# Graph aggregation with the weighting matrix as the stationary operand: node sums on the lanes, copied by ScalarE and transposed back, in groups of 896 edges with matrices of 128 columns

## The reference, cut to what matters

```python
def _gcn_layer(x, W, b, edge_weight, edge_src, edge_dst):
    support = x @ W
    msgs = support[edge_src] * edge_weight[:, None]
    agg = jax.ops.segment_sum(msgs, edge_dst, num_segments=N_NODES)
    return agg + b
h = jax.nn.elu(_gcn_layer(x, W1, b1, edge_weight, edge_src, edge_dst))
h = jax.nn.elu(_gcn_layer(h, W2, b2, edge_weight, edge_src, edge_dst))

...
x = x + _L0_gnn_ref(_layernorm(x, axis=-1), L0_gnn_W1, L0_gnn_b1, L0_gnn_W2, L0_gnn_b2, edge_weight, src, dst)
x = x + _L0_ffn_ref(_layernorm(x, axis=-1)[None], L0_ffn_W1, L0_ffn_b1, L0_ffn_Wg, L0_ffn_bg, L0_ffn_Wd, L0_ffn_bd)[0]
```

## Time and profile before

| | us |
|---|---|
| median of 3 runs | 4540.26 (4538.99 to 4540.56) |
| profiled execution, first to last instruction (span) | 5639.2 |
| profiled execution, anything around the span | not given |
| PE busy, share of the span | 3611.2, 64% |
| POOL busy, share of the span | 3287.1, 58% |
| DVE busy, share of the span | 2125.6, 38% |
| ACT busy, share of the span | 1218.9, 22% |

### The profile page before, as it was taken

The page is one execution under the profiler, slowest core; times in us unless marked ns, Lnnn a source line. Parts: engine busy times, 40 slices in busy tenths (PEclk is TensorE's granted clock), DMA queues, the critical chain, the costliest instruction groups (busy, mean ns, idle before and its releaser), DMA issues.

```text
span 5639.2 us, 84567 instructions
## 1 busy us (share of the span) xinstructions
PE 3611.2 (64%) x21407; PEld 3303.4 (59%) x21408; DVE 2125.6 (38%) x7215; ACT 1218.9 (22%) x2041; POOL 3287.1 (58%) x3464
## 2 busy tenths in 40 slices
PE   4555445555555545557667676666776776678998
PEld 3554444555544545456666666666666666667777
DVE  6663233223232322224334443333443433354332
ACT  4551110000000000013223232232232322232111
POOL 5666556666666666655565655555555555524555
PEclk6666666666666666668777777778777777789999
DMA  4543323333333333323333333333333333344444
GB/s 149 166 154 92 90 86 91 95 96 93 96 95 96 94 96 93 94 77 103 104 115 113 114 114 114 106 108 111 113 112 110 111 111 104 107 130 142 156 156 138
DMA packets 248031, 626.81 MB, mean 111 GB/s; under 512 B 66279, under 2 KB 113014, under 8 KB 247358
## 3 DMA queue, kind: packets, MB, share of 16 engines
q0 software_dynamic: 173664, 491.88, 30.3%
q1 hardware_dynamic: 69646, 103.75, 5.1%
q10 hardware_dynamic: 4176, 26.61, 1.3%
HBM read 519.22 MB, written 103.73 MB: 110 GB/s over the span
## 4 chain that ended last, share of the span: by engine, by line
PE 40%; issue 24%; another core or an unknown queue 4%; DVEq 4%; DVE 3%; DMA 2%; ACT 1%; POOL 0%; POOLq 0%; ACTq 0%; SPq 0%
PE pA L1381 18%; PE pB L1422 13%; PE pZ L1391 3%; PE pC L1404 3%; DMA aggT<-pay_scratch,ids 2%; PE pA L1536 1%; DVE S L927 1%; DVEq L927 1%; PE pZ L1415 1%; DVEq L953 1%; PE pT L1410 0%; DVE aggT L978 0%; PE pC L1526 0%; DVEq L978 0%
## 5 line engine op out<-in xcount | busy, mean ns | idle before, releaser
L1381 PE MATMUL pA<-S,rows 128*128 128x96 f32 x12544 | 1857.1, 312 | 961.7 <-issue 639.8
L1381 PEld LDWEIGHTS pA<-S,rows 128*128 128x128 f32 x12544 | 1797.0, 228 | 1039.1 <-issue 1033.8
L549 POOL DMA_INDIRECT rows<-h_scratch,idx x1564 | 1491.4, 954 | 1107.8 <-issue 424.2
L549 POOL DMA_INDIRECT rows<-xn_scratch,idx x1296 | 1227.9, 947 | 742.7 <-issue 366.2
L1422 PE MATMUL pB<-work,w 128*128 128x128 f32 x3232 | 776.5, 380 | 707.3 <-issue 702.3
L1422 PEld LDWEIGHTS pB<-work,w 128*128 128x128 f32 x3232 | 656.0, 279 | 818.9 <-issue 818.2
L927 DVE TENSOR_SCALAR S<-iota_p,tdst,twgt 128x96 f32<-128x96 f32 x3168 | 852.8, 351 | 288.2 <-issue 280.7
L978 DVE TENSOR_TENSOR aggT<-aggT,pA 128x192 f32 x784 | 278.0, 355 | 1340.3 <-remote 851.1
L1030 DVE TENSOR_TENSOR zb<-pZ,brow 128x256 f32<-128x256 f32 x198 | 84.0, 424 | 1150.0 <-issue 692.8
L1391 PE MATMUL pZ<-wg,stage 128*128 128x256 f32 x784 | 276.0, 485 | 213.0 <-ACT stage L642 126.2
L1536 PE MATMUL pA<-aggT,work 128*128 x1680 | 387.5, 384 | 10.8 <-DVE work L1311 10.1
(11 more groups left out here) (200 smaller groups left out, 2613.9 us busy)
## 6 DMA issues: line engine op xcount, KB each, us to landing
pay_scratch<-work SPq DMA_DIRECT2D x98, 512.0 KB
rows<-h_scratch,idx POOLq DMA_INDIRECT x1564
rows<-xn_scratch,idx POOLq DMA_INDIRECT x1296
work<-in_x_dram ACTq DMA_DIRECT2D x15, 896.0 KB
xn_scratch<-work ACTq DMA_DIRECT2D x14, 896.0 KB
h_scratch<-work SPq DMA_DIRECT2D x98, 128.0 KB
pay_scratch<-work SPq DMA_DIRECT2D x98, 128.0 KB
work<-in_x_dram SPq DMA_DIRECT2D x97, 128.0 KB
```

The costliest lines, as they stand in the source:

```text
L549: pool.indirect_dma_start(rows[:, s, t, :], None, source, bass.IndirectOffsetOnAxis(at, 0))\
L1381: last = mm(to[:, k * W:(k + 1) * W], rows[:, slot, t, k * P:(k + 1) * P], Sx[:, t, :], start=(t == 0), stop=(t == T - 1))
```

## The change

- Groups have 7 tiles (896 edges), 224 per layer; a half is 2 groups, 112 halves per layer; 4 slots for gathered rows instead of 8. The matrices have 128 columns.
- In the product `S` is the stationary operand and the gathered rows stream past, 256 columns, so the sums have nodes on the lanes (`group_products`). Both groups of a half share a bank of `pA`.
- ACT copies the sums of a half from PSUM to `gsum`, 512 columns (`copy_sums`), before its ticks; in the raw stage behind the normalising of the next half's rows. PE turns them with four transposes into the other bank of `pA` (`transpose_sums`), behind the half's ticks. DVE adds them to `aggT`, one instruction of 256 columns per group (`add_groups`).
- DVE builds the matrices of the next half ahead of its ticks, from a small copy of the table's columns (`tnext`), made two halves ahead, without register offsets.
- In the raw stage statistics, root, scales and normalising go by half (14 tiles) instead of by pair (8 tiles).
- At most `0.875 h + 3` blocks are due by half h (`PACE`).
- Tables of the start have rows of 896 edges, in two chunks of up to 128 groups instead of four.

The diff, cut to its core. The sizes, and ACT's part (the raw stage, the copy, the order behind the raw stage):

```diff
-    T = 4
+    T = 7
     GE = T * P
-    W = 96
-    SLOTS = 8
+    W = P
+    SLOTS = 4
+    PACE = 0.875
...
             def raw_half(i, half, with_chunk):
...
-                row_root(2 * h + 2, ahead)
-                row_normalise(2 * h + 2, ahead)
+                row_root(h + 1, ahead)
+                row_normalise(h + 1, ahead)
+                copy_sums(0, h)
                 if with_chunk:
                     chunk_normalise(h, half)
                     chunk_store(h, half)
                     chunk_root(h + 1)
-                row_root(2 * h + 3, ahead + 2)
-                row_normalise(2 * h + 3, ahead + 2)
...
+            def copy_sums(layer, h):
+                act.wait_ge(s_mm[layer], HALF * h + HALF + SLOTS)
+                act.activation(gsum[:, :], pG2, ACT.Copy).then_inc(s_gc[layer], 1)
...
                     for half in range(2):
                         h = 2 * i + half
+                        copy_sums(layer, h)
                         _, start, end = half_flags(act, layer, h)
                         ticks(act, start, end, lambda j: (tick1, tick2)[layer](j, h))
```

DVE's part (matrices, adds, the order in the raw stage and behind it):

```diff
+            def build_S(layer, h, buf):
+                dve.wait_ge(s_tab[layer], h + 1)
+                for u in range(HALF):
+                    dve.wait_ge(s_mm[layer], HALF * h + u + (SLOTS - HALF + 1))
+                    for t in range(T):
+                        last = v.tensor_scalar(S[:, u, t, :], iota_w[:, :], tnext[:, buf, 0, t, u:u + 1],
+                                               tnext[:, buf, 1, t, u:u + 1], ALU.is_equal, ALU.mult)
+                    last.then_inc(s_S[layer], 1)
...
+            def add_groups(layer, h):
+                bases = bases_of(h)
+                dve.wait_ge(s_tr[layer], h + 1)
+                for u in range(HALF):
+                    hold(dve, s_add[layer], HALF * h + u + HALF)
+                    to = aggT[:, :, bass.ds(bases[u], W)]
+                    v.tensor_tensor(to, to, pSUM[:, u * C:(u + 1) * C].rearrange("p (k n) -> p k n", k=KC), ALU.add)\
+                     .then_inc(s_add[layer], 1)
...
-                        for u in range(0, HALF, 2):
-                            pair = 2 * h + 2 + u // 2
-                            row_statistics(pair, ahead + u, value)
-                            bases = pair_ready(0, h, u)
-                            add_group(0, h, u, bases[0])
-                            row_scales(pair, ahead + u)
-                            add_group(0, h, u + 1, bases[1])
-                            next_matrices(0, h, u)
-                            if with_chunk and u == 0:
-                                chunk_statistics(h + 1, 1 - half)
+                        row_statistics(h + 1, ahead, value)
+                        row_scales(h + 1, ahead)
+                        build_S(0, h + 1, 1 - half)
+                        if with_chunk:
+                            chunk_statistics(h + 1, 1 - half)
+                        add_groups(0, h)
                         if with_chunk:
                             chunk_scales(h + 1)
+                        copy_columns(0, h + 2, half)
...
+                        build_S(layer, h + 1, 1 - half)
                         ticks(dve, start, end, (tick1, tick2)[layer])
-                        for u in range(0, HALF, 2):
-                            bases = pair_ready(layer, h, u)
-                            for n in range(2):
-                                add_group(layer, h, u + n, bases[n])
-                            next_matrices(layer, h, u)
+                        add_groups(layer, h)
+                        copy_columns(layer, h + 2, half)
```

PE's part:

```diff
+            def group_products(slot, u):
+                for t in range(T):
+                    last = mm(pG2[:, u * C:(u + 1) * C], S[:, u, t, :], rows[:, slot, t, :],
+                              start=(t == 0), stop=(t == T - 1))
+                return last
+
+            def transpose_sums(layer, h):
+                pe.wait_ge(s_gc[layer], h + 1)
+                pe.wait_ge(s_add[layer], HALF * h + HALF)
+                for u in range(HALF):
+                    for k in range(KC):
+                        at = u * C + k * P
+                        last = nc.tensor.transpose(pSUM[:, at:at + P], gsum[:, at:at + P], ident[:, :])
+                last.then_inc(s_tr[layer], 1)
...
                     pe.wait_ge(s_S[layer], g + 1)
-                    if u % 2 == 0:
-                        pe.wait_ge(s_add[layer], g + 2)
-                    products(half * HALF + u, S[:, u, :, :], group_sum(u), s_mm[layer])
+                    group_products(half * HALF + u, u).then_inc(s_mm[layer], 1)
                 if not raw:
                     ticks(pe, start, end, tick)
+                transpose_sums(layer, h)
```

More of the change, by code:

```diff
@@ L246, in bass_gnn_then_routed_ffn @@
         pF = pC[:, :].rearrange("p (b n) -> p b n", b=2)[:, :, 0:PERB * PG].rearrange("p b (c g) -> p b c g", g=PG)
[L247 to L251 removed]
+        pLG = pZ[:, C:C + NX]
+        pG2 = pA[:, 0, :]
+        pSUM = pA[:, 1, :]
+        assert HALF * C <= 512 and KC * W == C and 2 * C <= 512
         block = ctx.enter_context(nc.Block())
@@ L291, in bass_gnn_then_routed_ffn @@
         s_mm = [sem(f"group_multiplied_{l}") for l in range(2)]
+        s_gc = [sem(f"group_sums_copied_{l}") for l in range(2)]
+        s_tr = [sem(f"group_sums_transposed_{l}") for l in range(2)]
+        s_tab = [sem(f"table_columns_copied_{l}") for l in range(2)]
         s_add = [sem(f"group_added_{l}") for l in range(2)]
@@ L725, in _ @@
             act.sem_inc(s_xst, 1)
-            for pair in range(HALF // 2):
-                row_root(pair, 2 * pair)
+            row_root(0, 0)
             row_normalise(0, 0)
             chunk_root(0)
-            row_normalise(1, 2)
             def raw_half(i, half, with_chunk):
@@ L866, in _ @@
             LO4 = LOr[:, 0:NG].rearrange("o (h g) -> o h g", g=HALF)
-            for r in range(2):
+            for r in range(HALF // 2):
                 pair = regs[0:1, 0:NH, 1 + r]
@@ L921, in _, with copy_columns @@
             dve.wait_ge(s_aggclear, 3)
-            def build_S(layer, g, half):
-                dve.wait_ge(s_mm[layer], g + (SLOTS - HALF + 1))
-                for t in range(T):
-                    last = v.tensor_scalar(S[:, half, t, :], iota_w[:, :], tdst[:, t, bass.ds(g, 1)],
-                                           twgt[:, t, bass.ds(g, 1)], ALU.is_equal, ALU.mult)
-                last.then_inc(s_S[layer], 1)
+            def copy_columns(layer, h, buf):
+                v.tensor_copy(tnext[:, buf, :, :, :], tab[:, :, :, bass.ds(h * HALF, HALF)]).then_inc(s_tab[layer], 1)
+            def build_S(layer, h, buf):
[6 more added lines that the diff above has]
+                    last.then_inc(s_S[layer], 1)
             def overflow(layer, g, base):
@@ L1106, in _ @@
                         stage_idx(layer, at, at)
+                    tc.then(v.memset(pB[:, T * P:1024], 0.0))
                     tc.then(v.memset(pC[:, :], 0.0))
                 dve.sem_inc(s_add[layer], HALF)
-                for u in range(HALF):
-                    build_S(layer, u, u)
+                for buf in range(2):
+                    copy_columns(layer, buf, buf)
+                build_S(layer, 0, 0)
                 if layer == 0:
-                    for pair in range(HALF // 2):
-                        row_statistics(pair, 2 * pair, 16 * T)
-                    for pair in range(HALF // 2):
-                        row_scales(pair, 2 * pair)
+                    row_statistics(0, 0, 16 * T)
+                    row_scales(0, 0)
                     chunk_statistics(0, 0)
```

83 lines of the change are left out of this document (32 added, 51 removed).

## The result

Four runs of each kernel, on one chip: before 4539.77 us (4538.99 to 4540.56), after **4633.77 us** (4633.25 to 4637.54). The ratio is **1.0207, 95% interval 1.0193 to 1.0222**: 94 us slower. The direction and the range held (4535 to 4700); of the size, 36.5 us, only two fifths were forecast.

What follows compares the result with a forecast made beforehand. POOL's gather pace of 1.25 us was taken to bound both layers, unprofiled. Terms -2.5 (gathers) + 25 + 8 + 6 = +36.5 us gave 4577 us; range 4535 to 4700, the forecast's own 4555 to 4610.

Steps and rivals of the forecast that it cites:

- Products: Group products on PE: 2 passes of 256 columns per 128 edges, 0.45 or 0.86 us, beside gathers, 0 us.
- Transposes and copy: Per half, four PE transposes of 0.5 us and one ACT copy of 0.60 us; their cost is counted by stage.
- Matrices: DVE builds 14 per half, 3.5 to 4.7 us of 17.5; 0 us, but the tick waits behind them.
- Raw stage: Start of layer 0: slot chain of 20.7 us against 17.5, paid by every second half, +25 us (0 to +50).
- Start: Before the first product: five gathers fewer ahead, but more statistics, tiles and passes; +8 us (0 to +15).
- Layer 0 behind it: Layer 0 after the raw stage: PE needs 10.5 or 17.6 us of 17.5, slots give 17 us slack; 0 us.
- Layer 1: PE needs 16.8 us of 17.5 in a half with a tick, mean 15.6; POOL still leads, 0 us.
- Ends: Last group of each layer: wider passes, then copy and transposes before the add; +3.6 and +2.5, +6 us.
- A: Rival: PE sets the pace, so half the group instructions makes it faster, 4493 us; chance 0.15.
- B: Rival: no change, as the raw chain stays under 17.5 us at full clock, 4545 us; chance 0.20.
- C: Rival: layer 1 turns PE-led as waits lower PE's clock, +100 us, 4677 us; chance 0.15.
- What would show it: Signs: 3126 gathers at 1.25 us, raw waits every second half, PE idle some 3 us, span falling more than time.

Runs made afterwards that it cites:

- account of before: Profile of the kernel before with the second feature half multiplied for one of a group's four tiles, 3 of 8 products left out; 4537.34 us beside 4539.24.

## Why the prediction was right or wrong

**The bound** was right: POOL's gathers set the pace of both layers (1.25 us; 3126 gathers). Removing 3 products of 8 gained nothing, and freeing PE of 265 us of waiting gained 10. Its reading of the 0.70 us steps as something that timed runs lack was right for these runs only; on the second kind of chip they are in the timed runs.

**Gathers, Products, Transposes and copy, Matrices** came as costed: -2 gathers; 28 passes in 6.21 us (0.222 each) at a granted clock of 1.00; four transposes 0.60; copy 0.60; seven matrices 1.88. PE's wait ahead of the tick's first product was 2.84 us, where 3.2 were forecast:

```profile
3004.57 0.17 DVE L1061 TENSOR_TENSOR LG<-lgpart 128x8 f32 x1 [0.17 <-DVE lgpart L1059]
...
3004.79 3.09 PE L1417 MATMUL pC<-identg,work 128*128 128x136 f32 x12 [2.84 <-DVE LG L1061]
```

**Raw stage, +25: the term that failed.** Layer 0 cost 54.8 us, of which about 7 belongs to the start and 47 to the raw stage. The step took one chain, slot to slot over two halves, 3.2 us over for every second half. It left out the chunk (its 7 tiles, store, root and scales), which makes the chain close on itself within one half: 20.8 us against 17.5, paid by every half; 14 halves x 3.3 = 46. The wrong chain was the error, and with it half the halves; the cure shows it: with the chunk and the blocks taken apart, 53 us of layer 0 came back. That the wrong chain (20.7) and the right one (20.8) are equally long is luck: they share statistics, root, normalising and copy, but one has landing, transposes and products where the other has the chunk. The step's upper end, +50 if every half pays, covers what was measured, but the forecast did not go by it.

**Start, +8:** 2.6 at the first gather and one gap of 7.6 that ends at 60 us, against none in the account of before: 10. Near enough. (The stop of 12.4 us is of the second kind of chip.)

**Layer 0 behind it, 0:** held.

**Layer 1, 0:** PE stayed covered, as forecast, but the layer is 14.5 us longer. 2.9 us is one wait, and the rest is gathers held by a sum of two tiles in SBUF: 86 instead of 31, 0.24 us each, 55 x 0.24 = 13. Together that is 16 against 15.7 by the column "over". The prediction had no term for it: it took a gather's length as fixed, whatever VectorE does beside it. The order of VectorE's work decides how many gathers start just behind such a sum; that it happened so often in the changed kernel is its phase against the gathers, and no run tells more.

**Ends, +6:** 3.9 at the joint and 11.3 behind, 15. The step counted the last products, copy and transposes. It left out that PE takes the half's tick between them: at the end of layer 1 the last products end 7.8 us behind the last gather's start, the tick's passes follow to 17.4, the transposes start at 17.5 and the last adds at 18.5, against 5.6 in the account of before. The last adds of layer 0 start at 12.2 us against 5.7. So three ticks of layer 1 stand behind the last gather instead of two, and the expert loop starts 11.8 us later (119.6 against 107.8). No run tried another order here; with VectorE's tick first the part behind did not shrink (590.5).

Of the rivals, **A** fell with fewer products. It rested on the shares of a profile of the second kind; in the account of before, PE's loads are busy 61% of the span and POOL 72%, so there the shares point to POOL themselves. **B** fell with the raw stage. **C** is not what happened here, for POOL's waits in layer 1 are 2.9 us; but its mechanism, a changed kernel without cover for a slower PE, is what the second kind of chip shows. **What would show it** came true, except for the raw gaps in every half; the span fell far more than the time (by 1008 us), though because the two profiles are of two kinds of chip.

## What to carry to other kernels

When buffers are regrouped, compare two numbers: the time that the stock of buffers lasts at the leader's pace, and the longest closed loop through all engines, small root-and-scale steps of side work included; here the stock per half fell from 20 to 17.5 us and the loop came to 20.8. An order of instructions that was harmless under the old stock (a chunk's scales at the end of a half) must be looked at anew. A probe that adds an instruction to a long loop can cost its reloading instead of itself: look at the instruction queue's packets before reading the time. And count what an effect needs (here a start within 0.3 us behind a sum), not only how often it occurs: the bare number of long gathers hid the effect that the probe was for.

## What the runs showed of the hardware

- Chips of one type run the kernel before at 4540 or at 5620 us, three seen of each. The second shows up as PE instructions 0.7 us and more apart by "issue"; there the same change costs 7.7% instead of 2.1%.
- One instruction more in the tick made VectorE's loop of layer 1 be loaded anew each pass: 310 packets instead of 34, and a stop of 6.7 us a pass (352.6 us in 53).
- An indirect gather of 0.95 us that starts 0.05 to 0.3 us behind the start of a VectorE sum of two operands in SBUF (0.42 us) takes between 1.20 and 0.98 us, the less the later it starts; from 0.3 us on it takes 0.95 again. In layer 1 of the nine profiles of the first kind 457 gathers start 0.05 to 0.27 us behind such a sum and 456 of them take over 1.0 us; of the other 13,611 two take over 1.08 us.
